# Zero-mean down weights and late shared tiles summed in PSUM, in a one-core attention and mixture-of-experts kernel

## What is computed

```
x = x + layernorm(attention(layernorm(x)))     # 16 heads, 4 kv heads, width 128, causal, rotary, norm on q and k
x = x + layernorm(ffn(layernorm(x)))

ffn(x):
  probs   = softmax(x @ gate_w.T);  top 2 of 8 experts, weights renormalised
  out     = sum over the 2 experts: weight * ((silu(x @ w_gate[e]) * (x @ w_up[e])) @ w_down[e])      # hidden 176
  sgate   = sigmoid(x @ shgate_w)
  sh      = (silu(x @ shw_gate) * (x @ shw_up)) @ shw_down                                            # hidden 352
  return out + sgate * sh

layernorm(x) = (x - mean(x)) / sqrt(var(x) + 1e-5)
```

## Time and profile before

| | |
|---|---|
| median of three runs | 668.02 us (667.78 to 670.14) |
| the profiled execution: its time, its span | 673.56 us, 671.8 us |
| TensorE busy | 631.1 us, 94% |
| ScalarE, VectorE, GpSimd busy | 551.3 us (82%), 549.9 us (82%), 530.5 us (79%) |
| first load of routed results issued | 640.4 us |
| last shared down projection (tile 15) begins | 653.5 us |
| last VectorE instruction begins | 666.9 us |

### The profile page before, as it was taken

How to read it: one execution, slowest core, us unless ns; L and a number is a source line. 1 busy time by engine, 2 the same in 40 slices (tenths; PEclk the granted TensorE clock), 3 DMA queues, 4 the chain that set the end, 5 groups by cost and what they waited for, 6 DMA issues and landing times.

```text
span 671.8 us, 15617 instructions
## 1 busy us (share of the span) xinstructions
PE 631.1 (94%) x4506; PEld 586.9 (87%) x4506; DVE 549.9 (82%) x1912; ACT 551.3 (82%) x2105; POOL 530.5 (79%) x601
## 2 busy tenths in 40 slices
PE   5879999999999999999999999999789989999993
PEld 5657899999999999999999999999678889999991
DVE  3989999898898889899898999979878755555466
ACT  3589999999999999999999999999787536666633
POOL 3698898999899899989989998999757424666664
PEclk9999999999999999999999999999899999999997
DMA  8001306997740000000000000000526033444173
GB/s 328 33 0 33 104 1 198 335 335 209 4 47 1 1 1 1 1 1 2 1 1 1 1 1 2 1 1 25 160 101 229 33 90 111 128 130 119 67 265 125
DMA packets 51122, 54.27 MB, mean 81 GB/s; under 512 B 19840, under 2 KB 42752, under 8 KB 50912
## 3 DMA queue, kind: packets, MB, share of 16 engines
q1 hardware_dynamic: 47632, 43.90, 23.6%
q0 software_dynamic: 3408, 9.38, 3.7%
HBM read 23.83 MB, written 29.51 MB: 79 GB/s over the span
## 4 chain that ended last, share of the span: by engine, by line
PE 75%; DVE 9%; POOL 5%; issue 4%; ACT 4%; DMA 2%; POOLq 0%; SPq 0%; ACTq 0%; DVEq 0%
PE pQ L470 8%; PE pQ L471 8%; PE pQ L472 8%; PE pPO L576 5%; PE pPO L470 5%; PE pPO L472 5%; PE pPO L471 5%; PE pT L548 4%; PE pSS L470 3%; PE pA L470 3%; PE pA L471 3%; PE pA L472 3%; PE pSS L471 2%; PE pSS L472 2%; POOL xs L2076 2%
## 5 line engine op out<-in xcount | busy, mean ns | idle before, releaser
L1002 ACT ACTIVATE P<-P,nmx 128x128 f32<-128x128 f32 (+1 forms) x256 | 118.8, 491 | 1.0 <-DVE nmx L1445 1.0
L470 PE MATMUL pQ<-W 128*128 128x512 f32 (+2 forms) x334 | 116.1, 347 | 2.4 <-DVE W L1359 1.2
L471 PE MATMUL pQ<-W 128*128 128x512 f32 (+2 forms) x334 | 111.6, 334 | 0.0
L472 PE MATMUL pQ<-W 128*128 128x512 f32 (+2 forms) x334 | 111.3, 333 | 0.0
L1982 POOL TENSOR_TENSOR ropes<-ropes 128x640 f32<-128x640 f32 x63 | 99.3, 1576 | 13.7 <-DVE ropes L1422 13.4
L1010 ACT ACTIVATE P<-P,rinv 128x128 f32<-128x128 f32 (+1 forms) x256 | 105.8, 481 | 2.1 <-DVE rinv L1451 2.1
L1992 POOL TENSOR_TENSOR ropes<-ropes 128x640 f32<-128x640 f32 x63 | 99.6, 1580 | 4.9
L470 PE MATMUL pPO<-W 128*128 128x256 f32 (+1 forms) x323 | 95.3, 295 | 5.6 <-DVE W L1460 3.9
L987 ACT ACTIVATE ropes<-pQ 128x128 f32<-128x128 f32 x320 | 88.4, 303 | 9.7 <-PE pQ L472 9.7
L471 PE MATMUL pPO<-W 128*128 128x256 f32 (+1 forms) x323 | 92.0, 285 | 0.0
L472 PE MATMUL pPO<-W 128*128 128x256 f32 (+1 forms) x323 | 91.8, 284 | 0.0
(11 more groups left out here) (272 smaller groups left out, 2170.5 us busy)
## 6 DMA issues: line engine op xcount, KB each, us to landing
xs<-stage SPq DMA_DIRECT2D x1, 17550.0 KB, 58.4
stage<-xs SPq DMA_DIRECT2D x39, 130.0 KB
ropes<-in_ew SPq DMA_DIRECT2D x8, 608.0 KB
stage<-in_wqkv SPq DMA_DIRECT2D x3, 768.0 KB, 9.0
stage<-ys SPq DMA_DIRECT2D x4, 512.0 KB, 7.3
ropes<-ys SPq DMA_DIRECT2D x4, 512.0 KB, 6.8
out<-X SPq DMA_DIRECT2D x7, 256.0 KB, 2.0
X<-in_wo SPq DMA_DIRECT2D x1, 1536.0 KB, 12.7
```

The costliest lines, as they stand in the source:

```text
L470: e.matmul(out, lh, rh, start=start, stop=False, skip_group_check=True)
L471: e.matmul(out, lh, rl, start=False, stop=False, skip_group_check=True)
L472: return e.matmul(out, ll, rh, start=False, stop=stop, skip_group_check=True)
L1002: a = e.activation(P[:, z, span(t)], P[:, z, span(t)], ACT.Exp, bias=nmx[:, z, t:t + 1], scale=-1.0, accum_out=sums[:, z, t:t + 1])
```

## The change

The down weights are made to have zero mean in every row of 256, once, on the chip: in the attention loop SyncE loads ten pieces of them (up to 128 x 512), VectorE sums each row and subtracts the mean, and SyncE stores the piece in a new HBM buffer `downs`, from which the weights are later loaded. A token's ffn output then has mean zero, so the last layer norm needs only the sum of squares. Shared tiles 12 to 15 have their gate folded into the hidden product and project straight into the PSUM bank in which their pair's routed results were summed. Pair 5 moves from TensorE to GpSimd and VectorE (`PPE` = 6).

```diff
+DOWN = [(x, EA, EH) for x in range(NE)] + [(NE, 0, 2 * HID), (NE, 2 * HID, NKT * HID)]
+DOWN_SUM = {56 + 6 * c: c for c in range(len(DOWN))}
+DOWN_SUB = {58 + 6 * c: c for c in range(len(DOWN))}
-PPE = 5
-PSUM = U1 + NT - UFIRST + 1
+PPE = 6
+NSUM = 2 * PPE
...
-        pSum = [pS[1], pA, pT]
+        pSum = [pS[1], pA]
...
@@ SyncE
+            load_down(0)
+            for c in range(len(DOWN)):
+                x, a, b = DOWN[c]
+                e.wait_ge(s_down, 2 * c + 1)
+                if c > 0:
+                    e.wait_ge(s_sdown, 16 * c)
+                if c + 1 < len(DOWN):
+                    load_down(c + 1)
+                e.wait_ge(s_down, 2 * c + 2)
+                e.dma_start(downs_d[:, c * 512:c * 512 + b - a], down_raw[c % 2][:, 0:b - a]).then_inc(s_sdown, 16)
             e.wait_ge(s_swlo, 2)
-            e.dma_start(sw_raw[2], sw_d[:, 2 * SHUP:]).then_inc(s_dsw, 16)
+            e.wait_ge(s_sdown, 16 * len(DOWN))
+            e.dma_start(sw_raw[2], downs_d[:, NE * 2 * HID:]).then_inc(s_dsw, 16)
...
-                e.dma_start(ew_raw[x % 3], ew_d[:, x * EH:(x + 1) * EH]).then_inc(s_dew[x % 2], 16)
+                e.dma_start(ew_raw[x % 3][:, 0:EA], ew_d[:, x * EH:x * EH + EA]).then_inc(s_dew[x % 2], 16)
+                e.dma_start(ew_raw[x % 3][:, EA:EH], downs_d[:, x * 512:x * 512 + 512]).then_inc(s_dew[x % 2], 16)
...
-            for p in range(NPAIR):
-                if p == 6:
-                    e.wait_ge(s_hU, NOWN)
+            e.wait_ge(s_hU, NOWN)
+            for p in (0, 1, 6, 2, 3, 7, 4, 5):
                 e.dma_start(yl[p], ...)
@@ TensorE
+                out = pair_row[m // 2][:, m % 2, :] if m >= NSUM else pD      # u_down
...
-                if q == PSUM:
-                    pair_results(PPE)
                 if before2 == "U" and q > U1:
+                    if g >= NSUM and g % 2 == 0:
+                        pair_results(g // 2)
                     u_down(g)
...
-                if q == PSUM:
-                    pair_shared(PPE)
-                    for p in range(PPE + 1, NPAIR):
-                        pair_results(p)
-                        pair_shared(p)
@@ ScalarE
-            def last_apply(p):                  # two ACTIVATE Identity with scale and bias
+            def last_square(p):
...
+                    a = e.activation(yl[p][:, t, HID:2 * HID], pair_row[p][:, t, :], ACT.Square,
+                                     accum_out=mv2[:, p % 4, t, 1:2])
+                if q in PAIR:
+                    last_square(PAIR[q])
@@ VectorE
+            def down_mean(c):
+                e.tensor_reduce(down_sum[:, c, 0:n], rows_c, AXX, ALU.add).then_inc(s_down, 1)
+            def down_centre(c):
+                e.scalar_tensor_tensor(rows_c, down_sum[:, c, 0:n].unsqueeze(2).to_broadcast([128, n, HID]), -1.0 / HID,
+                                       rows_c, ALU.mult, ALU.add).then_inc(s_down, 1)
...
-                e.tensor_tensor(actb[m % 2][:, 0:NSH], sgb[m % 2], pU, ALU.mult).then_inc(s_uact, 1)
+                    e.scalar_tensor_tensor(actb[m % 2][:, 0:NSH], sgb[m % 2], sgate[:, m:m + 1], pU, ALU.mult,
+                                           ALU.mult).then_inc(s_uact, 1)          # m >= NSUM
...
-            def last_stats(p): ...              # bn_stats, bn_aggr
-            def last_scale(p): ...
+            def last_add(p):
+                    a = e.scalar_tensor_tensor(x, pair_row[p][:, t, :], lr2[:, p % 4, t:t + 1], x, ALU.mult, ALU.add)
@@ GpSimd, last_root
-                if p < NPAIR - 1:
-                    e.tensor_scalar(nb2[:, z, :], mv2[:, z, :, 0], -1.0, None, ALU.mult)
...
-                    e.tensor_tensor(nb2[:, z, :], nb2[:, z, :], lr2[:, z, :], ALU.mult).then_inc(s_nb2, 1)
```

More of the change, by code:

```diff
@@ L202, in program @@
         rw_raw = rc[:, 215:215 + 2 * NR].rearrange("p (k r) -> p k r", k=2)
+        down_raw = [part(ropes, 2304 + 512 * z, 512) for z in range(2)]
         ew_raw = [part(ropes, z * EH, EH) for z in range(3)]
@@ L319, in program @@
                              "s_rhi"))
-        s_shared, s_y, s_fapp = (sem(n) for n in ("s_shared", "s_y", "s_fapp"))
+        s_shared, s_y, s_ssq = (sem(n) for n in ("s_shared", "s_y", "s_ssq"))
         s_bn, s_aggr, s_hrow, s_hT, s_wqlo, s_tab_d, s_rope_d = (
@@ L693, in u_down @@
                     e.wait_ge(s_osb, NB)
-                else:
+                elif m < NSUM:
                     e.wait_ge(s_shared, m)
@@ L697, in u_down @@
                     e.wait_ge(s_y, NRT)
+                out = pair_row[m // 2][:, m % 2, :] if m >= NSUM else pD
                 for k in range(NKT):
-                    p = mm3(pD, [aTs[m % 2][:, i, k * 128:k * 128 + 128] for i in range(2)],
-                            [shdown_w(i, k) for i in range(2)], k == 0, k == NKT - 1)
+                    p = mm3(out, [aTs[m % 2][:, i, k * 128:k * 128 + 128] for i in range(2)],
+                            [shdown_w(i, k) for i in range(2)], k == 0 and m < NSUM, k == NKT - 1)
                 p.then_inc(s_udown, 1)
@@ L769, in pair_results @@
                     e.wait_ge(s_y, NRT)
-                elif p == PPE + 1:
+                else:
                     e.wait_ge(s_rlo, NRT)
-                else:
-                    e.wait_ge(s_usilu, NT)
                 e.matmul(pair_row[p], ident, yl[p][:, :, 0:HID], start=True, stop=False, skip_group_check=True)
                 e.matmul(pair_row[p], ident, yl[p][:, :, HID:2 * HID], start=False, stop=False, skip_group_check=True)
-            def pair_shared(p):
-                e.wait_ge(s_shared, 2 * p + 2)
-                e.matmul(pair_row[p], ident, shpair[p].rearrange("p (t c) -> p t c", t=2), start=False, stop=True,
-                         skip_group_check=True).then_inc(s_psum, 1)
             def ffn(q):
@@ L1138, in r_out @@
                 e.activation(yb[j % YRING], pY[j % 2], ACT.Copy, scale=wsel[:, j % 16:j % 16 + 1]).then_inc(s_y, 1)
-            def last_apply(p):
-                e.wait_ge(s_nb2, NB + root_of(p) + 1)
+            def last_square(p):
+                if p < PPE:
+                    e.wait_ge(s_fsum, p + 1)
+                else:
+                    e.wait_ge(s_udown, 2 * p + 2)
+                if p < 4:
+                    e.wait_ge(s_nb2, NB)
+                else:
+                    e.wait_ge(s_lr2, NB + root_of(p - 4) + 1)
                 for t in range(2):
-                    a = e.activation(yl[p][:, t, 0:HID], pair_row[p][:, t, :], ACT.Identity, bias=nb2[:, p % 4, t:t + 1],
-                                     scale=lr2[:, p % 4, t:t + 1])
-                a.then_inc(s_fapp, 1)
+                    a = e.activation(yl[p][:, t, HID:2 * HID], pair_row[p][:, t, :], ACT.Square,
+                                     accum_out=mv2[:, p % 4, t, 1:2])
+                a.then_inc(s_ssq, 1)
             def ffn(q):
@@ L1160, in ffn @@
                     u_silu(i)
-                if before2 == "U" and q > U1:
+                if before2 == "U" and q > U1 and g < NSUM:
                     u_out(g)
@@ L1172, in ffn @@
                         r_hi(h)
-                p = PAIR.get(q - 1, 0)
-                if 0 < p < 6 and p % 2 == 1:
-                    last_apply(p - 1)
-                    last_apply(p)
-                elif p == 6:
-                    last_apply(p)
+                if q in PAIR:
+                    last_square(PAIR[q])
             e.wait_ge(s_dgb, 16)
@@ L1556, in u_act @@
                     e.wait_ge(s_uT, m - 1)
-                e.tensor_tensor(actb[m % 2][:, 0:NSH], sgb[m % 2], pU, ALU.mult).then_inc(s_uact, 1)
+                if m < NSUM:
+                    e.tensor_tensor(actb[m % 2][:, 0:NSH], sgb[m % 2], pU, ALU.mult).then_inc(s_uact, 1)
+                else:
+                    e.wait_ge(s_shalf, 1 if m < 14 else 2)
+                    e.scalar_tensor_tensor(actb[m % 2][:, 0:NSH], sgb[m % 2], sgate[:, m:m + 1], pU, ALU.mult,
+                                           ALU.mult).then_inc(s_uact, 1)
             def u_lo(m):
@@ L1766, in ffn @@
                     last_add(p)
-                elif p == 6:
+                elif p >= 6:
                     last_add(p)
-                elif p == 7:
-                    last_scale(p)
-                    for t in range(2):
-                        last_add_tile(p, t)
             ln1_stats(0)
@@ L1820, in _ @@
                     router_constants()
+                if s in DOWN_SUM:
+                    down_mean(DOWN_SUM[s])
+                if s in DOWN_SUB:
+                    down_centre(DOWN_SUB[s])
                 if s == 108:
```

59 lines of the change are left out of this document (24 added, 35 removed).

## The result

The changed kernel takes 675.28 us (median of 6 runs, 673.82 to 677.33) against 668.47 us for the kernel before in the same session (6 runs, 667.78 to 670.14). The ratio is 1.0092, 95% interval 1.0075 to 1.011, which is 6.1 us. In a later session it was 675.28 us again, ratio 1.0082 (1.0062 to 1.0101). The prediction said 670.6 us, at most 674.5. It was wrong in size, not in sign.

The account below looks back on a forecast made before the run. TensorE was taken to bound the attention, and a ladder of VectorE, GpSimd and ScalarE hand-overs the tail. Attention +2.0 and tail +0.6 gave +2.6 on 668.0, so 670.6 us, range 665.0 to 674.5.

Parts of the forecast that it names:

- The load of the pieces: Attention: each piece's load is free; the first has about 15 us before its sum at step 56.
- The length of the new operations: VectorE in attention: a sum takes 0.65 us, a centring 1.3 us (rows from 0.68 to 1.66).
- The slack: Attention: 1.5 us fit an ordinary step's end, 0.8 behind statistics; three centrings behind statistics cost 0.5 each, 1.5 us.
- The piece at the routing: Attention steps 110 and 112: VectorE is full there, so the last piece costs 0.5 us, ends 0 and 1.9.
- attention: Whole attention stretch: the added sums and centrings make it 2.0 us longer, ends 0 and 4.5.
- The transfers: Expert weights in 16 transfers instead of 8, same bytes: 0 us, +0.5 at most.
- TensorE's pause: Tail, before tile 12's down projection: TensorE waits 2.5 us for pair 6's results, the third load.
- the whole tail: From TensorE's late work to the last add: +0.6 us, bounds -2.5 and +3.
- The ladder behind tile 15's low part: Tail: sums, squares, roots and adds up to the last VectorE instruction take 9.5 us instead of 14.2.
- rival A: Tail: TensorE's clock falls in the new pause, +1.7 us, 672.3 us in all; chance 0.28.
- B: Attention: VectorE and GpSimd hold each other up at all ten centrings, 6.5 us instead of 2.0, 675; chance 0.10.
- C: Early third load takes 2.5 us off the tail, centrings at 0.68 another 2.0: 666.1; chance 0.22 for 664 to 668.

Follow-up runs that it names:

- centre_moved: Changed kernel with its sums and centrings at other steps, the first sum at step 48, before its piece could be there; 692.16 us, ratio 1.035.
- after_again: The changed kernel run again unchanged in a later session; 675.28 us, ratio 1.0082 to the kernel before.
- six_first: Changed kernel with only SyncE's loads of routed results reordered, pair 6's first and pair 7's fourth; 671.68 us, ratio 1.0034.
- free_six: Changed kernel with sums and centrings moved off statistics and routing steps, none before step 56, and pair 6's results loaded first; 668.96 us, ratio 1.0006.
- centring_only: Kernel before plus down pieces loaded, summed, centred, stored and loaded again, keeping its own tail; 676.25 us, ratio 1.0057.
- no_centring: Changed kernel with all transfers, but the ten sums and ten centrings replaced by one-column copies; 676.25 us, ratio 1.0056.
- tail_only: Kernel before with the changed kernel's tail alone, no down pieces and no centring; 676.55 us, ratio 1.0054.
- centre_scalar: Changed kernel with each centring done by a small 128x2 operation and one tensor_scalar per row of 256; 690.64, 692.81 and 700.44 us, ratio 1.038.
- before_again: The kernel before, unchanged, for a second trace, timed against itself; 673.2 us, ratio 0.9999.

## Why the prediction was wrong

*The load of the pieces: right.* No sum waited; centre_moved shows what eight steps earlier cost.

*The length of the new operations: nearly right.* 0.65 forecast for the sum, 0.68 measured. For the centring 1.3, and 1.0 at the median, from 0.66 to 1.79. Of 0.68 and 1.33 in the earlier trace rows I had to choose; both are there, by whether GpSimd works beside it.

*The slack: right, but used with a mean.* The 1.5 us of an ordinary step's end and the 0.8 behind statistics hold about: 1.74 in an ordinary step cost nothing, 2.02 cost 1.1. I took 1.3 for every centring, so 0.5 for each of the three behind statistics. They took 1.79, 1.72 and 0.66: on the mean 1.39, nearly as forecast, but what counts is the part above 0.8. That is 1.0, 0.9 and nothing, 1.9 in place of 1.5. If the 0.3 by which each long one holds up GpSimd's next operation comes on top, it is 2.5, and 2.5 were measured (1.4 and 1.1); that it does is my reckoning, no run has it apart. Where the length has two values and the slack lies between them, each value has to be charged apart.

*The piece at the routing: wrong in its mechanism.* I had 0.5 for the lateness that the piece's own 0.65 and 1.3 would add. It lasts 0.39 and 0.41 and costs nothing by itself. What costs 1.3, or nothing in after_again, are two older routing operations that GpSimd now holds up. So attention comes to +2.4 to +3.8; 2.0 was forecast and 4.5 was the bound. By the ratios, with what else those kernels differ in, it is 1.9 us (six_first against free_six, two sessions, by their intervals 0.6 to 3.1) to 3.8 (centring_only).

*The transfers: right*, nothing (no_centring).

*TensorE's pause: right*, 2.57 for 2.5, and without the fall of the clock the whole tail is +0.9 (tail_only) where +0.6 was forecast. The ladder behind tile 15's low part is 9.56 for 9.5, in part by luck, since VectorE's adds of pairs 4 to 6, which I had not chained, take as long as the roots.

**The step that failed** is the choice that the clock stays up behind the new pause. I gave rival A a chance of 0.28 and left its 1.7 us out of the forecast. It fell in five of the six profiles that have the pause (centre_moved's and centre_scalar's show 0.50 too), for 1.3 to 1.7 us; A's price was right, its chance too low. The earlier trace rows showed a fall behind 2.81 and none behind 1.76, and 2.57 lies nearer to the first. Even that one fall was a matter of the execution: behind the same pause of 2.81 the clock fell in ten of fourteen profiles. The rows of one trace could not tell this; a second trace of the kernel before would have. What decides it in one execution, no run shows. The Trainium skill ("TensorE: Matmul & The Clock Gate", section "What's actually happening") has the clock halved after an idle window whose place is not tied to the work; the runs agree in that the same program had the fall in one execution and not in the other (before and before_again).

**The second step that failed**, missing from the sum: the program's end, 1.2 us more between VectorE's last add and the end of the span. I had followed the chain of waits to the last add and put what lies behind at no change, without a reason.

So 2.0 + 0.6 = 2.6 became 2.4 to 3.8 for attention, 0.9 for the pause, 1.4 for the clock, 1.2 for the end and -0.6 for the routed tiles: 5.3 to 6.7, and 6.1 and 5.5 are what the two ratios say. The clock and the end erred by 1.4 and 1.2 us and the attention by 0.4 to 1.8, all to the same side. The upper end of the range, 674.5, had room for rival A (672.3) and for an attention of 3.8 instead of 2.0: together 674.1. The end's 1.2, the pause's 0.3 and the routed tiles' -0.6 make it 675.0, and 675.28 was measured. By this reckoning it was the end, which no rival held, that put the time outside.

*Rivals B and C.* B had GpSimd and VectorE in each other's way at all ten centrings; it happens at five of them and reaches TensorE at two, and, which I had not thought of, at two operations of the routing. C's condition, an early load of pair 6, is what six_first makes, and it gives 3.2 us by the pause (1.8; C had 2.5) and the clock (1.4).

## What to carry to other kernels

A VectorE instruction that is kept apart from GpSimd's should be one long one, placed where the step's slack holds its longest length, not its mean; two tables of step numbers were worth 1.9 us here by the ratios and 3.7 in the attention of the two traces. It can also move an old, short instruction behind one of GpSimd's, so look at those beside it. Where TensorE is made to wait for a transfer, order the transfers by the first use: one tuple was worth 3.2 us. And when TensorE gets a new pause of a length behind which its clock has fallen, put the lower clock into the forecast and not among the rivals: behind the two pauses of 2.2 to 2.8 us followed here, the old one and the new, it fell fifteen times in twenty. Last, what lies behind the last instruction belongs in the sum too; it was 1.2 us here.

## What the hardware showed unexpectedly

- A tensor_scalar on 128x2 values in SBUF, 147 ns alone, lasted 1.09 us at the median and 1.43 at most in centre_scalar's trace, beside GpSimd's operations. The one-column copies in no_centring, in the same places, lasted at most 0.15.
- A tensor_tensor on 128x80 values with two tensor inputs from SBUF lasted 0.24 us when it started 0.02 us ahead of GpSimd's operation and 1.65 us when it started 0.02 us behind, in two executions of one program; with what follows it is 1.3 us of the kernel's time.
- The granted clock fell behind the pause before pair 6's products in five of six profiles, at pauses of 2.20 to 2.71 us, and stayed at 1.00 in the sixth, at 2.33. Behind a pause of 2.81 to 2.83 us that all profiles share it fell in ten and not in four, and of the two executions of the kernel before in one.
- The same program, run again, took 0 or 2.6 us longer between attention and routed tiles.
- SyncE's wait for TensorE's queue at the program's end was 1.9, 2.1 or 3.1 us, the same in every profile of one program, and not set by TensorE's count of matmuls.
